# The last chunk of a mixture-of-experts layer: routed group in place of the dense form

## The chip, the cores and the metric

The kernel runs on one core of a Trainium2 chip. The metric is the device time of one execution in microseconds (us). Before the change the median of three executions is 1103.75 us (1101.72 to 1103.85).

## The reference

One transformer layer in float32 on x of 4 x 1024 tokens x 256 dims: causal attention over a window of 64 tokens (16 heads of 16 dims), residual and layernorm, then a mixture of experts, residual and layernorm.

```python
x = layernorm(x + attention(x))                      # x: (4, 1024, 256)
scores = sigmoid(x @ router_weight.T)                # 16 experts
sc = scores + e_bias                                 # top 2 of 4 groups, then
tidx = top_k(masked sc, 4)[1]                        # top 4 experts of a token
tw = 2.5 * scores[tidx] / sum(scores[tidx])
h = silu(x @ gate_w[e].T) * (x @ up_w[e].T)          # 256 -> 128, per expert
routed = sum over the 4 experts of tw * (h @ down_w[e].T)
shared = silu(x @ sg.T) * (x @ su.T) @ sd.T          # 256 -> 2 x 128
x = layernorm(x + routed + shared)
```

## The kernel before, in words

The 4096 tokens are 8 chunks (c) of 512 tokens, a chunk is 4 tiles of 128. Attention runs as 16 rounds of 13 slots. A planner, `plan()`, written in Python, gives every other job an integer half slot h on each of the five engines; each engine runs its jobs in order of h (`PE_AT`, `ACT_AT`, `DVE_AT`, `POOL_AT`, `SP_AT`) and waits on semaphores in between. Nothing is reordered at run time: a job that waits holds all that stands behind it on its engine. From `tail` = 416 on there are no attention slots, and the engines run only this list. Slots below are given relative to `tail`.

The experts are computed for groups of tokens. Groups 0, 1 and 2 are a batch of 8 tiles each, and group 3 is chunk 6 with 4 tiles. A routed group goes through these steps:

- `route` (5 parts) and `place` (5 parts) on DVE: top 4 of the experts and a row number for each of the token's four copies. Between them a `pos` job on PE (counts of tokens before each token).
- `scatter` on POOL: one indirect DMA per tile and rank, 16 for a group of 4 tiles, 32 for 8. It writes rows of the token in float16 pairs (high and low) into `rows[g % 2]` in DRAM. It waits until the last `gu` of group g - 2, which used the same buffer, is done.
- `load_rows` on SP: a transposing DMA of 256 rows, a pair of units. A unit is 128 rows of one expert; a group has 4 units per tile and 16 more for the rounding up, so 48 or 32 units, 24 or 16 pairs.
- `gu` on PE: 24 matmuls of 128 columns for a pair (gate and up, each in three float16 products). `tanh` (ACT), `gate` (DVE), `hh` (ACT) and `hl` (DVE) make the float16 pair of h, then `y` on PE: 6 matmuls of 256 columns. The planner puts `y` 7 slots behind its `gu` and holds five such pairs between them.
- `y_out` on ACT (into one of three `ys` buffers), `store_y` on SP into `outs[g % 2]` in DRAM.
- `gather` on POOL: one indirect DMA per tile and rank. It waits for all stores of its group, and for `comb_done` of the tile two before it, as there are two buffers `yg`.
- `combine` (4 dependent operations on a tile) and `stats2` on DVE; for each chunk `aggr2` (DVE), `rstd2` (POOL), `norm2` (ACT), `store` (SP).

The two shared experts of a group are `gu` and `ysh` jobs of 256 columns that need no scatter: they read `x1h` and `x1l` directly.

The last chunk, c = 7 (`DENSE`), is not routed to units: each of its tokens goes through all 16 experts and the 2 shared ones. `up` n is 12 matmuls of 512 columns, `dsilu`, `dgate` (times the weight of the expert, which `load_c` has spread over the partitions from `c_dram`), `dhi`, `dlo`, then `down` n, 12 matmuls of 256 columns that accumulate in two PSUM banks over all 18 experts. `residual` adds the sum to x1, and `aggr2` to `store` follow. There is nothing to scatter or to gather.

In the list the last `gu` of group 2 is at slot 38 and its last `y` at 45; group 3's routed pairs have `gu` from 48 to 83 and `y` from 55 to 90; `up` and `down` stand between them from 52 on, most of them behind; the gathers of group 2 are at 51 to 82 with `combine` at 58, 62, ... 86; those of group 3 are at 96 to 106. The list ends at slot 122.

Of the kernel before, what the change touches and what calls it, by code (L numbers as in the profile page):

```python
# [5 lines left out]
F32 = mybir.dt.float32  # L6
# [3 lines left out]
ALU = mybir.AluOpType  # L10
# [35 lines left out]
GROUPS = [(b, 0, BT) for b in range(B - 1)] + [(B - 1, 0, NT)]  # L46
DENSE = NC - 1
# [21 lines left out]
NCB = 4  # L69
NDH = 4  # L70
LAG = 2
# [43 lines left out]


def down(pe, dve, pool, act, sp, put, downs, h, w):

    n = downs.pop(0)
    h = put(("down", n), h)  # L120
    if n == NX - 1:
        at = max(h, w)
        dve[at + 1].append(("residual",))
        dve[at + 2].append(("aggr2", DENSE))
        pool[at + 3].append(("rstd2", DENSE))
        act[at + 4].append(("norm2", DENSE))
        sp[at + 5].append(("store", DENSE))
    return h


def plan():
# [40 lines left out]
    def chain(c, o, gap):  # L172
# [128 lines left out]
LO_POOL = ()  # L301
# [21 lines left out]
def attention_moe(nc, x, xT, winT, bqkT, bvr, woutT, bout, rwT, ebias, gwT, uwT, dwT, sgT, suT, sdT, out):  # L323
    with ExitStack() as ctx:
# [6 lines left out]
        c_dram = nc.dram_tensor("c_dram", [NE, CH], F32).ap()  # L331
# [11 lines left out]
        program(nc, ctx, banks, att, proj, moe, q_dram, k_dram, v_dram, c_dram, x1_dram, rows, outs, x, xT, winT, bqkT, bvr, woutT,  # L343
# [102 lines left out]
def program(nc, ctx, banks, att, proj, moe, q_dram, k_dram, v_dram, c_dram, x1_dram, rows, outs, x, xT, winT, bqkT, bvr, woutT, bout,  # L446
            rwT, ebias, gwT, uwT, dwT, sgT, suT, sdT, out):

    def sems(names, prefix):
# [23 lines left out]
    d = sems("""c_done cT_ready cT_done c_written c_loaded0 c_loaded1 c_loaded2 c_loaded3 up_ready silu_done sc_done h_done  # L473
        hi_done lo_done down_done z_done""", "d_")
    c_loaded = [d[f"c_loaded{i}"] for i in range(NCB)]
# [14 lines left out]
    cb = [flat[0].bitcast(F32)[:, i * CH:i * CH + CH] for i in range(NCB)]  # L490
    dhh, dhl = ([flat[1][:, (NDH * part + i) * CH:(NDH * part + i) * CH + CH] for i in range(NDH)] for part in range(2))
    cT = flat[2].bitcast(F32)[0:NE, 0:CH]
    dq, dga = ([PT[part][:, i, :] for i in range(2)] for part in range(2))
    dhf = [PT[part][:, 2, :] for part in range(2)]
# [3 lines left out]
    def rows_in(i):  # L498

        if i < LATE:  # L500
# [4 lines left out]
    cw = pick[:, DENSE % NH2 * NT:DENSE % NH2 * NT + NT, 0, :]  # L505
# [8 lines left out]
    RINGS = {"s_first": [0, 1, 2], "st_first": [3, 4, 5], "first": [7], "scores": [0, 1, 2, 3, 4], "other": [5, 7], "project": [5, 6, 7], "gates": [0, 1], "ups": [2, 3],  # L514
             "end": [5, 7, 0, 1, 2, 3], "sum0": [4], "sum1": [6]}
# [37 lines left out]
    def emptied(job):  # L553
# [49 lines left out]
    with nc.Block() as block:  # L603

        @block.tensor
        def _(pe):
# [97 lines left out]
            experts, sums = {}, []  # L704
# [14 lines left out]
            def fill(h):  # L719
# [59 lines left out]
                elif what == "cT":  # L779
                    on.wait_ge(d["c_done"], 1)  # L780
                    ps = take(ring, "cT")
                    for j in range(NT):
                        mm = pe.transpose(ps[0:NE, j * P:j * P + P], cw[:, j, :], ident[:])
                    mm.then_inc(d["cT_ready"], 1)
                elif what == "up":
                    n, = a
                    e, at = NE + n if n < NSH else n - NSH, DENSE % NH2 * CH
                    on.wait_ge(*x1_halves(DENSE))
                    on.wait_ge(s["w_lo"], NX)
                    for up, name in enumerate(("gates", "ups")):  # L790
                        ps = take(ring, name, n)
                        i = 0
                        for lo, xx in ((0, x1h), (0, x1l), (1, x1h)):
                            for k in range(KD):
                                mm = pe.matmul(ps[:], weights(e, (2 * up + lo) * D + k * P, P), xx[:, k, at:at + CH],  # L795
                                               start=(i == 0), stop=(i == 5))
                                i += 1
                        mm.then_inc(d["up_ready"], 1)
                elif what == "down":
                    n, = a  # L800
                    e = NE + n if n < NSH else n - NSH
                    on.wait_ge(d["lo_done"], n + 1)
                    if n == 0:
                        on.wait_ge(s["ot_done"], NR * NH2)
                        sums[:] = [take(f"sum{i}", "sum", i) for i in range(2)]
                    for j in range(NT):
                        y = sums[j // 2][:, j % 2 * D:j % 2 * D + D]
                        for i, (o, at) in enumerate(((dhh, 4 * D), (dhh, 5 * D), (dhl, 4 * D))):
                            mm = pe.matmul(y, o[n % NDH][:, j * P:j * P + P], weights(e, at, D),
                                           start=(n == 0 and i == 0 and j % 2 == 0), stop=(n == NX - 1 and i == 2),  # L810
                                           skip_group_check=True)
# [946 lines left out]
```

## Time and profile before

| what | us |
|---|---|
| median of three executions | 1103.75 |
| the profiled execution | 1103.76 |
| its span in the trace | 1102.0 |
| PE busy | 994.0 (90%) |
| DVE busy | 826.5 (75%) |
| ACT busy | 622.2 (56%) |
| POOL busy | 464.1 (42%) |

The device time of the profiled execution is 1.76 us above its span. A busy PE is not PE at its peak, since matmuls are pipelined and each is shown until it has drained. The profile gives for each line of the kernel and engine how long it was busy, and what ended the idle time before it. Instructions that issue a DMA from SP or POOL are shown with the time of the issue, not of the transfer.

### The profile page before, as it was taken

Reading aid. Unit: us, or ns where it says so; the run is one execution under the profiler, and the core shown is the slowest. Engines: PE = TensorE matmul, PEld = TensorE weight load, DVE = VectorE, ACT = ScalarE, POOL = GpSimd, SP = SyncE. Lnnn points to the kernel's source line nnn. Section 1 sums busy time; section 2 is a strip of 40 time slices with the busy share of each in tenths; the row PEclk is TensorE's granted clock in tenths of the full one; section 3 lists DMA queues with packets and bytes.
Section 4 is the critical chain, followed back from the end, with each engine's and each line's share of the span. In section 5 each row is a group of like instructions: output and inputs, shape, how many; then the busy total and the mean of one; then the engine's idle time right before and its main releaser. Section 6 shows DMA issues by size and latency. Waiting matters only on the chain.

```text
span 1102.0 us, 24714 instructions
## 1 busy us (share of the span) xinstructions
PE 994.0 (90%) x8538; PEld 574.0 (52%) x8538; DVE 826.5 (75%) x1824; ACT 622.2 (56%) x1418; POOL 464.1 (42%) x679
## 2 busy tenths in 40 slices
PE   8999999988888999998899988997998967999994
PEld 4554444444433455565564545564664546777662
DVE  8778888877887777778877888689776658457583
ACT  4336878676545666665466557664555754444322
POOL 8752221242128504120475665211556754246351
PEclk9999999999989999999999999999999988999997
DMA  5863356643113443543283866451446745899541
GB/s 186 264 220 98 125 176 212 224 119 83 49 43 112 110 97 92 115 116 65 83 183 125 174 154 160 80 119 40 119 153 134 200 108 158 185 196 239 179 140 39
DMA packets 216662, 150.73 MB, mean 137 GB/s; under 512 B 134608, under 2 KB 192720, under 8 KB 216544
## 3 DMA queue, kind: packets, MB, share of 16 engines
q1 hardware_dynamic: 204160, 116.63, 41.3%
q0 software_dynamic: 10752, 29.37, 8.7%
q10 hardware_dynamic: 1632, 3.15, 0.8%
q8 instruction: 75, 1.23, 0.5%
q14 instruction: 43, 0.35, 0.1%
HBM read 52.46 MB, written 70.29 MB: 111 GB/s over the span
## 4 chain that ended last, share of the span: by engine, by line
PE 53%; DVE 23%; POOL 6%; DMA 5%; issue 5%; ACT 5%; SPq 2%; DVEq 0%; ACTq 0%; POOLq 0%
PE bank L839 12%; PE bank L659 11%; PE bank L629 9%; PE bank L642 9%; DVE a_mx L1385 7%; DVE e_R L1679 4%; PE bank L852 3%; DMA a_pool<-outs,e_slot 2%; DMA k_dram<-p_qk 2%; PE bank L632 2%; PE bank L864 1%; PE bank L745 1%; ACT a_PT L1247 1%; POOL rows L1178 1%; ACT e_R L1301 1%
## 5 line engine op out<-in xcount | busy, mean ns | idle before, releaser
L1385 DVE TENSOR_REDUCE a_mx<-bank 128x1 f32<-128x512 f32 (+3 forms) x720 | 421.0, 618 | 140.1 <-PE bank L632 86.4
L1247 ACT ACTIVATE a_PT<-bank 128x512 f32<-128x512 f32 (+4 forms) x832 | 373.1, 497 | 176.8 <-PE bank L642 173.0
L642 PE MATMUL bank<-a_QS,a_KS 113*128 113x512 f16 (+4 forms) x832 | 272.0, 335 | 14.1 <-DVE a_mx L1385 13.3
L629 PE MATMUL bank<-a_KS,a_QS 112*128 112x512 f16 (+4 forms) x832 | 260.6, 334 | 13.9 <-DVE a_mx L1385 9.1
L1136 POOL TENSOR_SCALAR_AFFINE_SELECT a_PT<-a_PT 128x256 f32<-128x256 f32 (+1 forms) x288 | 112.2, 397 | 319.5 <-ACT a_PT L1247 318.8
L659 PE MATMUL bank<-a_PT,a_VG 128*17 128x512 f32 (+4 forms) x1664 | 182.7, 511 | 5.0 <-POOL a_PT L1136 4.9
L1178 POOL DMA_INDIRECT rows<-e_XR,e_slot x112 | 111.3, 993 | 108.2 <-DVEq L1537 80.0
L1186 POOL DMA_INDIRECT a_pool<-outs,e_slot x112 | 111.2, 993 | 84.5 <-DMA outs<-e_ys 32.6
L629 PEld LDWEIGHTS bank<-a_KS,a_QS 112*128 112x128 f16 x832 | 79.9, 98 | 114.0 <-ACT a_PT L1247 54.9
L642 PEld LDWEIGHTS bank<-a_QS,a_KS 113*128 113x128 f16 x832 | 81.1, 99 | 89.3 <-DVE a_mx L1385 35.2
L1331 ACT ACTIVATE e_tq<-bank 128x256 f32<-128x256 f32 x116 | 44.5, 384 | 143.2 <-PE bank L839 140.9
L839 PE MATMUL bank<-e_xt,a_W 128*128 128x128 f16 x1416 | 107.9, 225 | 8.4 <-DVE e_hf L1622 6.9
L632 PE MATMUL bank<-a_tri,a_idb 128*128 128x128 f16 (+1 forms) x576 | 110.6, 211 | 0.0
L839 PEld LDWEIGHTS bank<-e_xt,a_W 128*128 x1416 | 91.6, 100 | 29.7 <-issue 17.7
L852 PE MATMUL bank<-a_W,e_hh 128*128 x352 | 63.2, 276 | 7.5 <-DVE e_R L1669 3.4
L632 PEld LDWEIGHTS bank<-a_tri,a_idb 128*128 128x128 f16 x576 | 55.1, 99 | 27.8 <-issue 1.5
L1679 DVE SCALAR_TENSOR_TENSOR e_R<-a_pool,e_wk,e_R 128x256 f32<-128x256 f32 x112 | 57.8, 516 | 11.0 <-DMA a_pool<-outs,e_slot 8.0
L659 PEld LDWEIGHTS bank<-a_PT,a_VG 128*17 128x17 f32 x1664 | 33.8, 117 | 58.2 <-issue 45.3
L1629 DVE TENSOR_TENSOR e_hl<-e_hf,e_hh 128x256 f16<-128x256 f32 x116 | 49.7, 430 | 13.8 <-ACT e_hh L1338 11.8
L1338 ACT CAST e_hh<-e_hf 128x256 f16<-128x256 f32 x116 | 47.2, 408 | 19.3 <-DVE e_hf L1622 15.6
L1346 ACT ACTIVATE e_ys<-bank 128x512 f32<-128x512 f32 x88 | 52.2, 597 | 7.7 <-DMA outs<-e_ys 5.0
L795 PE MATMUL bank<-e_x1hl,a_W 128*128 128x512 f16 x216 | 49.4, 379 | 0.0
(178 smaller groups left out, 1323.6 us busy)
## 6 DMA issues: line engine op xcount, KB each, us to landing
outs<-e_ys SPq DMA_DIRECT2D x88, 256.0 KB, 3.8
rows<-a_pool SPq DMA_DIRECT2D x48, 256.0 KB, 3.6
q_dram<-p_qk SPq DMA_DIRECT2D x16, 256.0 KB, 2.8
k_dram<-p_qk SPq DMA_DIRECT2D x16, 256.0 KB, 4.0
v_dram<-p_vs SPq DMA_DIRECT2D x8, 512.0 KB, 7.3
a_QS<-q_dram SPq DMA_DIRECT2D x64, 64.0 KB
a_KS<-k_dram SPq DMA_DIRECT2D x64, 64.0 KB
a_VG<-v_dram SPq DMA_DIRECT2D x16, 256.0 KB, 4.2
```

What stands on the lines that cost most here:

```text
L629: mm = pe.matmul(ps[:, at:at + hi - lo], QS[p][0:MR, t // NT, h, t % NT * P:t % NT * P + P], KS[p][0:MR, piece, h % 2, 0:hi - lo], start=T ...
L632: mm = pe.matmul(ps[:, at + m0 - lo:at + hi - lo], idb[:], tri[:, m0 - P * t - WIN:m1 - P * t - WIN], start=False, stop=True)
L642: pe.matmul(ps[:, 0:(qc + 1) * CH - q0], KS[p][0:MR + 1, kt // NT, h % 2, kt % NT * P:kt % NT * P + P], QS[p][0:MR + 1, qc, h, q0 - qc * C ...
L659: mm = pe.matmul(otbank[32 * h:32 * h + HD + 1, q0 - qc * CH:CH], VG[p][:, kt, h:VW:HG], PT[(p + i) % 2][:, h, 0:(qc + 1) * CH - q0], star ...
L839: mm = pe.matmul(ps[:, up * 2 * P + at:up * 2 * P + at + v], weights(e, (2 * up + lo) * D + k * P, P), tall[k][part], start=(i == 0), stop ...
L852: mm = pe.matmul(ps[:, v * D:v * D + D], o[q % NHB][:, v * P:v * P + P], weights(e, at, D), start=(i == 0), stop=(i == 2))
L1136: pool.affine_select(out=a, in_=a, compare_op=ALU.is_ge, fill=0.0, base=q0 - (kt * P - WIN), pattern=[[0, 2], [1, w]], channel_multiplier= ...
L1178: pool.indirect_dma_start(rows[b % 2], bass.IndirectOffsetOnAxis(ap=slot[b % 3][:, at, k:k + 1], axis=0), XR[:, at, :], None).then_inc(sca ...
L1186: pool.indirect_dma_start(yg[i % 2][:, k, :], None, outs[b % 2], bass.IndirectOffsetOnAxis(ap=slot[b % 3][:, at, k:k + 1], axis=0)).then_i ...
L1247: act.activation(PT[(G + i) % 2][:, h, 0:w], bank("ST", G, i, h)[:, 0:w], ACT.Exp)\
L1385: dve.tensor_reduce(mx[:, piece, t // NT, heads[0]:heads[0] + n, t % NT], bank("S", G, u)[:, 0:n * w].rearrange("p (h k) -> p h k", h=n), ...
L1679: ins = dve.scalar_tensor_tensor(zz, yg[i % 2][:, k, :], wk[b % 3][:, at, k:k + 1], zz, op0=ALU.mult, op1=ALU.add)
```

## The change

Chunk 7 becomes group 4, a routed group of its own with 4 tiles in 32 units (16 pairs), built and run like group 3. The jobs `up`, `down`, `cT`, `dsilu`, `dgate`, `dhi`, `dlo`, `cTs`, `put_c`, `load_c`, `residual` and part 5 of `route` go, with their buffers and semaphores. Chunk 7 gets `row_hi` and `row_lo` (the float16 pair that is scattered), `pos`, `place`, scatters, gathers and combines. In the planner the routed pairs of group 4 are wanted only after the last one wanted of group 3, and the order of the jobs of groups 0 to 2 stays. The `end` ring of PSUM banks goes from six to seven.

```diff
-GROUPS = [(b, 0, BT) for b in range(B - 1)] + [(B - 1, 0, NT)]
-DENSE = NC - 1
+GROUPS = [(b, 0, BT) for b in range(B - 1)] + [(B - 1, half * NT, NT) for half in range(NH2)]
...
-        if c != DENSE:
-            act[y + 6].append(("row_hi", c))
-            pool[y + 7].append(("row_lo", c))
+        act[y + 6].append(("row_hi", c))
+        pool[y + 7].append(("row_lo", c))
...
-    sp[tail - 14].append(("load_res", DENSE))
-    pool[tail - 10].append(("add_bo", DENSE))
-    ready[DENSE], at = chain(DENSE, tail + 3, 1)
-    for n in range(RPARTS + 1):
-        dve[at + 2 + n].append(("route", NGR, n))
-    at = put(("cT",), at + RPARTS + 4)
-    act[at + 1].append(("cTs",))
-    sp[at + 2].append(("put_c",))
-    weighed = at + 3
-
     wanted, order = [], {}
+    for g in range(NGR):
+        lo = max(routed[g] + 5, max((h for h, *_ in wanted[-1:]), default=0) + 1 if g == NGR - 1 else 0)
+        hi = routed[g + 1] - 7 if g < B - 2 else LEFT + tail if g == B - 2 else lo + SPACE * NPR[g]
+        wanted += [(lo + (hi - lo) * n // NPR[g], g, NPS[g] + n) for n in range(NPR[g])]
     for g in range(NGR):
         for n in range(NPS[g]):
             c, tile = shared_place(g, n)
             wanted.append((ready[c] + tile * 5, g, n))
-        lo = routed[g] + 5
-        hi = routed[g + 1] - 7 if g < B - 2 else LEFT + tail if g == B - 2 else lo + SPACE * NPR[g]
-        wanted += [(lo + (hi - lo) * n // NPR[g], g, NPS[g] + n) for n in range(NPR[g])]
...
-    h, downs = ready[DENSE] + 1, []
-    for n in range(NX):
-        h = max(h + 1, ready[DENSE]) if n < NSH else max(h + 1, weighed + 1)
-        h = put(("up", n), h)
-        act[h + 1].append(("dsilu", n))
-        dve[h + 1].append(("dgate", n))
-        act[h + 1].append(("dhi", n))
-        (pool if n in LO_POOL else dve)[h + 2].append(("dlo", n))
-        if n >= NSH:
-            sp[h - 2 if n < NSH + NCB else h - 1].append(("load_c", n - NSH))
-        downs.append(n)
-        if len(downs) > LAG:
-            down(pe, dve, pool, act, sp, put, downs, h, w + 6)
-    while downs:
-        h = down(pe, dve, pool, act, sp, put, downs, h + 1, w + 6)
...
-    RINGS = {"s_first": [0, 1, 2], "st_first": [3, 4, 5], "first": [7], "scores": [0, 1, 2, 3, 4], "other": [5, 7], "project": [5, 6, 7], "gates": [0, 1], "ups": [2, 3],
-             "end": [5, 7, 0, 1, 2, 3], "sum0": [4], "sum1": [6]}
+    RINGS = {"s_first": [0, 1, 2], "st_first": [3, 4, 5], "first": [7], "scores": [0, 1, 2, 3, 4], "other": [5, 7], "project": [5, 6, 7], 
+             "end": [5, 7, 0, 1, 2, 3, 4]}
...
-                _, j0, n = GROUPS[r] if r < NGR else (B - 1, DENSE % NH2 * NT, NT)
+                _, j0, n = GROUPS[r]
```

## Rows read from the trace of the kernel before

**Rows 1.** Busy time of each engine by stretch, then PEclk, DMA share, GB/s.

```profile
900.00:905.00 5.00, 3.42 (x21) 3.02 (x20) 2.33 (x6) 3.92 (x8) 1.56 (x3) 0.50 0.26 82
...
980.00:1000.00 20.00, 19.44 (x199) 14.61 (x198) 12.28 (x29) 7.79 (x18) 9.54 (x11) 1.00 0.97 179
...
1040.00:1060.00 20.00, 19.52 (x121) 11.49 (x119) 14.18 (x24) 6.33 (x12) 11.83 (x11) 1.00 0.65 193
```

**Rows 2.** Waits from 940 to 1102 us: total, times, longest.

```profile
POOL a_pool L1186 <- DMA outs<-e_ys: 32.6, 2, 24.5
```

**Rows 3.** PE in order of time: start, length, line, shape, count, idle time before.

```profile
912.21 0.64 PE L852 MATMUL bank<-a_W,e_hh 128*128 x2
...
937.26 2.24 PE L839 MATMUL bank<-a_KS,a_W 128*128 128x128 f16 x24 [0.91 <-issue]
...
953.33 6.60 PE L839 MATMUL bank<-a_KS,a_W 128*128 128x128 f16 x72
...
968.48 1.50 PE L839 MATMUL bank<-a_PT,a_W 128*128 128x128 f16 x24
...
1028.13 1.47 PE L809 MATMUL bank<-a_W,a_QS 128*128 128x256 f16 x12
1029.44 2.75 PE L795 MATMUL bank<-e_x1hl,a_W 128*128 128x512 f16 x12
...
1032.58 0.27 PE L852 MATMUL bank<-a_W,e_hl 128*128 x1
```

**Rows 4.** POOL in order of time: scatters L1178, gathers L1186.

```profile
926.35 1.12 POOL L1178 DMA_INDIRECT rows<-e_XR,e_slot  x1 [0.75 <-DVEq L1537]
...
945.70 0.96 POOL L1178 DMA_INDIRECT rows<-e_XR,e_slot  x1 [0.30 <-issue]
971.17 0.98 POOL L1186 DMA_INDIRECT a_pool<-outs,e_slot  x1 [24.52 <-DMA outs<-e_ys]
...
1022.23 1.07 POOL L1186 DMA_INDIRECT a_pool<-outs,e_slot  x1 [0.30 <-issue]
...
1043.12 1.08 POOL L1186 DMA_INDIRECT a_pool<-outs,e_slot  x1 [8.04 <-DMA outs<-e_ys]
...
1066.46 0.95 POOL L1186 DMA_INDIRECT a_pool<-outs,e_slot  x1 [0.30 <-issue]
```

**Rows 5.** DVE in order of time: combines L1679.

```profile
1028.71 2.04 DVE L1679 SCALAR_TENSOR_TENSOR e_R<-a_pool,e_wk,e_R 128x256 f32<-128x256 f32 x4 [2.62 <-DMA a_pool<-outs,e_slot]
...
1053.58 2.04 DVE L1679 SCALAR_TENSOR_TENSOR e_R<-a_pool,e_wk,e_R 128x256 f32<-128x256 f32 x4
...
1070.90 2.04 DVE L1679 SCALAR_TENSOR_TENSOR e_R<-a_pool,e_wk,e_R 128x256 f32<-128x256 f32 x4
```

**Rows 6.** ACT in order of time: norm2 L1307, y_out L1346.

```profile
1035.11 2.08 ACT L1307 ACTIVATE e_R<-e_R,e_nm,e_rstd 128x256 f32<-128x256 f32 x4 [0.82 <-POOL e_nm L1147]
...
1039.67 0.59 ACT L1346 ACTIVATE e_ys<-bank 128x512 f32<-128x512 f32 x1
```

**Rows 7.** DVE in order of time, near the end: `bn_stats` of chunk 7.

```profile
1089.97 1.39 DVE L1662 BATCH_NORM_STATS2 e_st<-e_R 128x6 f32<-128x256 f32 x4
```

**Rows 8.** The page's costliest groups: `hh`, which stands for `tanh`, `gate` and `hl` too.

```profile
L1338 ACT CAST e_hh<-e_hf 128x256 f16<-128x256 f32 x116 | 47.2, 408 | 19.3 <-DVE e_hf L1622 15.6
```

**Rows 9.** Lines of `row_hi` and `row_lo`: duration min/median/max in ns, then first start.

```profile
L1281 ACT CAST e_XR<-e_R x7: 1027/1038/1067, 234.6 to 903.6; 128x1024 f16<-128x1024 f32 x7
...
L1168 POOL TENSOR_TENSOR e_XR<-e_R,e_XR x7: 2130/2132/2325, 236.7 to 904.7; 128x1024 f16<-128x1024 f32 x7
```

**Rows 10.** DMA queues from 980 to 1000 us: packets, MB, share of 16 engines.

```profile
q1 hardware_dynamic: 5974, 2.49, 67.6%
q0 software_dynamic: 379, 1.03, 28.7%
```

**Rows 11.** The same from 1043 to 1060 us.

```profile
q1 hardware_dynamic: 1064, 1.93, 37.6%
q0 software_dynamic: 473, 1.30, 25.4%
```

More of the change, by code:

```diff
@@ L114, in shared_place @@
     return chunk_of(g, n // NSH * 2), n // NSH * 2 % NT
[L117 to L128, printed above, removed]
 def plan():
@@ L300 @@
 SPACE = 2
-LO_POOL = ()
 PPARTS = 5
@@ L342, in attention_moe @@
         moe = expert_memory(opener(ctx, "e_"))
[L343 removed]
+        program(nc, ctx, banks, att, proj, moe, q_dram, k_dram, v_dram, x1_dram, rows, outs, x, xT, winT, bqkT, bvr, woutT,
                 bout, rwT, ebias, gwT, uwT, dwT, sgT, suT, sdT, out)
@@ L489, in program @@
     x1_loaded = [f["x1_loaded0"], f["x1_loaded1"]]
[L490 to L494, printed above, removed]
     late_tiles = [a.rearrange("p (k t) -> p k t", k=4) for a in (flat[2][:, 2 * CH:4 * CH], flat[3][:, 0:2 * CH],
@@ L778, in fill @@
                     mm.then_inc(f["pos_ready"], 1)
[L779 to L811, printed above, removed]
-                    mm.then_inc(d["down_done"], 1)
                 elif what == "gu":
@@ L1031, in fill @@
                           .then_inc(y_stored[i % 3], 16)
-                    elif what == "put_c":
-                        on.wait_ge(d["cT_done"], 1)
-                        sp.dma_start(c_dram, cT).then_inc(d["c_written"], 16)
-                    elif what == "load_c":
-                        e, = a
-                        on.wait_ge(d["c_written"], 16)
-                        on.wait_ge(s["st_ready"], (NR - 1) * NST)
-                        on.wait_ge(s["s_ready"], (NR - 1) * NU)
-                        on.wait_ge(d["sc_done"], e - NCB + 1)
-                        sp.dma_start(cb[e % NCB], c_dram[e, :].partition_broadcast(P)).then_inc(c_loaded[e % NCB], 16)
                     elif what == "store":
@@ L1491, in route @@
                                            op=ALU.is_equal))
-                    if r == NGR:
-                        link(dve.tensor_reduce(cw, kk.rearrange("p t k e -> p t e k"), AX.X, ALU.add))
-                        return
                     on.wait_ge(f["pos_ready"], r)
@@ L1630, in fill @@
                             .then_inc(f["hl_done"], 1)
-                    elif what == "dlo":
-                        n, = a
-                        on.wait_ge(d["hi_done"], n + 1)
-                        on.wait_ge(d["down_done"], n - NDH + 1)
-                        on.wait_ge(s["st_ready"], NR * NST)
-                        dve.tensor_tensor(dhl[n % NDH], dhf[n % 2], dhh[n % NDH], op=ALU.subtract)\
-                            .then_inc(d["lo_done"], 1)
-                    elif what == "dgate":
-                        n, = a
-                        on.wait_ge(d["silu_done"], n + 1)
-                        g = dq[n % 2]
-                        if n >= NSH:
-                            e = n - NSH
-                            on.wait_ge(c_loaded[e % NCB], (e // NCB + 1) * 16)
-                            on.wait_ge(d["h_done"], n - 1)
-                            g = dga[n % 2]
-                            dve.tensor_tensor(g, dq[n % 2], cb[e % NCB], op=ALU.mult).then_inc(d["sc_done"], 1)
-                            on.wait_ge(d["sc_done"], e + 1)
-                        on.wait_ge(d["up_ready"], 2 * n + 2)
-                        on.wait_ge(d["lo_done"], n - 1)
-                        dve.scalar_tensor_tensor(dhf[n % 2], bank("ups", n)[:], 1.0 / WSC, g, op0=ALU.mult, op1=ALU.mult)\
-                            .then_inc(d["h_done"], 1)
-                    elif what == "residual":
-                        on.wait_ge(d["down_done"], NX)
-                        for i in range(2):
-                            zz = x1_of(DENSE)[:, 2 * i:2 * i + 2, :].rearrange("p j n -> p (j n)")
-                            dve.scalar_tensor_tensor(zz, bank("sum", i)[:], 1.0 / WSC, zz, op0=ALU.mult, op1=ALU.add)\
-                               .then_inc(d["z_done"], 1)
-                        for i in range(2):
-                            on.wait_ge(d["z_done"], i + 1)
-                            for j in range(2 * i, 2 * i + 2):
-                                dve.bn_stats(st[1][:, j, :], x1_of(DENSE)[:, j, :]).then_inc(f["stats2_done"], 1)
                     elif what == "add_shared":
```

47 lines of the change are left out of this document (3 added, 44 removed).

## The prediction, made before the change was run

> **What bounds the kernel now.** The change touches nothing that is ordered before the last chunk's work, so I read only what lies behind 900 us, first by stage. The busy times say that PE is full and its clock is at the upper level from 980 to 1060 us, while the DMA share falls from 0.97 to 0.65 [rows 1]. Before that fall the routed pairs run, behind it the dense chunk, which needs little DMA. Next the waits: what the gathers on POOL wait for longest is the stores of `y`, 24.5 us before the gathers of group 2 and 8.0 before those of group 3 [rows 2, 4]. That idle time costs nothing now, because PE has the dense chunk to do: an `up` and a `down` take 1.31 + 2.59 us, read from the start of one to the start of the next [rows 3], and PE ends with them. Group 3's last `y` ends at 1032.85 [rows 3], its last combine at 1072.94 [rows 5], both in the shade of the dense work. So now the end is set by PE's matmuls, plus one short chain behind the last `down`: from the end of `bn_stats` at 1091.36 it is 10.6 us to the end of the span [rows 7].
>
> **The change, part by part.**
>
> *What goes.* 18 `up` and 18 `down` on PE, 18 x 3.9 = 70 us, and with them the DVE and ACT work per expert and the DMAs of 16 `load_c` and one `put_c`.
>
> *What comes on PE.* Four shared `gu` and two `ysh` of 12 matmuls of 256 columns. A `down` has the same form, 1.31 us, so 6 x 1.31 = 7.9. Then 16 pairs. A `gu` takes 2.2 us (72 matmuls in 6.60 for three) and at best, behind a backlog, 1.34 to 1.50 [rows 3]; a `y` is half a `down`, 0.66. From 937.26 to 959.93 there are eight `gu` and six `y`: 22.7 less 4.0 is 2.34 a `gu`, 3.0 a pair. 16 pairs are 48 us (bounds 32 and 48). PE thus saves 70 - 7.9 - 48 = 14 us. If PE still set the end, `y` of the last pair would be done at 968.5 (the start of group 3's first routed `gu` [rows 3]) + 8 shared jobs x 1.31 + 32 pairs x 3.0 = 1075.
>
> *What comes behind it.* A routed group ends with a store of `y`, a round of gathers, and combines. That is the serial part that the dense form did not have, and it is exposed at the end, as nothing is left to run beside it. The rest of the sum is a relay of three rounds, because POOL and DVE run their lists in order.
>
> 1. *Scatters of group 4.* They write to the buffer of group 2 and so wait for its last `gu`, which ends at 959.93 [rows 3]. POOL was idle there, from 946.66 to 971.17. Group 3's 16 scatters took 20.3 us [rows 4], so these end at 980.2, and the gathers of group 2, behind them on POOL, start 9 us later than their 971.17. All before 959.93 is covered: `route`, `pos` and `place` of group 4 run some 15 us earlier. `row_hi` and `row_lo`, 1.04 us on ACT and 2.1 on POOL [rows 9], fall before the idle stretch of POOL and cost nothing; without that cover they would be 3 us.
> 2. *Round of group 2.* First gather to last combine took 971.17 to 1030.75, 59.6 us [rows 4, 5]. POOL's own pace (31 intervals of 1.27, one `rstd2`, landing and combine) would give 48. I take 58, since the dense `dgate` and `dlo` no longer stand between the combines on DVE: 1038.2. `gate` and `hl` of the pairs wait behind these combines. By the planner's rule group 3's last `hl` now stands behind the last combine of group 2 (slots 89 and 86; before, both at 86, `hl` first). PE alone would be at that `y` about 1036, so DVE is late, not PE.
> 3. *To the gathers of group 3.* `norm2` of chunk 5 stands on ACT before the last two `y_out`. It ended 6.4 us behind the last combine of group 2 [rows 5, 6]; add 0.6 for one `y_out`, and 3.45 from the start of the last `y_out` to the first gather (1039.67 to 1043.12 [rows 4, 6]): 10.5, so 1048.7.
> 4. *Round of group 3*: 1043.12 to 1072.94, 29.8 us [rows 4, 5]. The arithmetic agrees: a tile is 4 gathers x 1.27, a combine came 6.5 us behind the start of its last gather where it waited for the DMA (1022.23 to 1028.71), and with two buffers that gives 29.9. It ends at 1078.5.
> 5. *Last pairs of group 4.* That combine is at slot 112, the `hl` of the last four pairs at 114 to 120. Again `norm2` (6.4), then `tanh`, `gate`, `hh`, `hl` at 0.41 [rows 8], `y` 0.66, `y_out` and store 3.45, and 0.5 for handoffs: 12.6, so 1091.1. PE alone would have let these gathers start at about 1079.
> 6. *Round of group 4.* Bounds 29.9 with the landing above and 25.7 with 4.4 us, the most that it can have been for group 3's last tile (1066.46 to 1070.90 [rows 4, 5]). The DMA queues are nearly idle by then, so 27: 1118.1.
> 7. *The end.* One `bn_stats` (0.42) and the 10.6: 11.1. Span 1129.2.
>
> The span of the profiled execution is 1.76 us short of its device time, which stands 0.01 above the median. So 1131.0, 27 us slower than 1103.75.
>
> The combine that waited for its DMA began 5.4 us behind the end of the issue (1023.30 to 1028.71 [rows 4, 5]). The Trainium skill, *DMA: Bandwidth & Descriptors*, section "Anatomy of one DMA — SWDGE (gpsimd) path", states a fixed cost of about 2.0 us plus the bytes; for 128 KB that is an estimated 2.3 us behind the issue, and by that estimate the last round would be 24.3 us and the whole 1128.
>
> **The rivals.**
>
> *Rounds at POOL's pace.* If landings are short, the round of group 2 takes 48 (1028.2), group 3's gathers start at 1038.7 and its combines end about 1064; then the relay has let go and PE's 1075 counts: + 3.6 + 25.7 + 11.1 = 1115.4, 1117 in device time. For it: only 4.4 us at most in the last round. Against it: combines of group 2 did wait for the DMA. The fixed cost that the Trainium skill gives on its DMA page, named above, would lead here too.
>
> *DMA becomes the bound.* From 1043 to 1060 eleven gathers took 25.4% and six loads of 256 KB 37.6% of 17 us, 0.39 and 1.07 us each [rows 11]. From 980 to 1000 the queue with six transposing loads and five plain transfers was busy 13.5 us [rows 10], so a transposing load is 1.36. Group 4's stage of some 48 us asks 16 x (1.36 + 1.07) + 16 x 0.39 and two outputs at about 2: 49 us. It is as full as the chip's queues go, and `y_out` waits for its buffer. If each round is longer by a tenth and the last pairs by 3 us, 1131 + 5.8 + 3 + 2.7 + 3 = 1145.
>
> *PE's clock falls.* At 900 to 905 PE was busy 3.42 of 5 us and the granted clock 0.50, that is 1.2 GHz; two matmuls of 256 columns then took 0.64 us in place of 0.38 [rows 1, 3]. With the dense work gone PE has pauses of that sort behind 1030. A `y` would be 1.3, a `gu` 2.6; twelve `gu` and sixteen `y` from 1040 end at 1092 instead of under the relay's 1087: 1136. The Trainium skill, *TensorE: Matmul & The Clock Gate*, section "What's actually happening", says that the throttled clock is the default and activity lifts it; the row at 900 us agrees, and by that rule the sum would be this 1136.
>
> *Faster.* The other side: no job waits behind a combine, and pairs run at 2.25 us, between the 2.0 of a backlog and 3.0. Then the last `y` is at 968.5 + 10.5 + 72 = 1051, and + 3.6 + 25.7 + 11.1 + 1.8 = 1093. This decides under 2.5 us a pair. For it: `gu` of 1.5 us do occur [rows 3]. Against it: those are behind an `up` or shared job, which gives the queue its backlog, and rounds at POOL's own pace with the handoffs between them give 1117 by themselves.
>
> **How the numbers follow.** The relay as summed 0.50 (1123 to 1138), POOL's pace 0.24 (1108 to 1122), DMA bound 0.13 (1138 to 1152), clock 0.06 (1136), faster 0.07, about half of it under 1101.5, the rest from there to 1108. The range that leaves out no more than 2 in 10 is 1108 to 1147. A measurement of this kernel tells 0.2%, 2.2 us, from no change. Faster by more 0.05, within 0.03, slower 0.92.
>
> **What would show it.** The first gather of group 2 at about 980 and 16 scatters before it; combines of group 3 ending near 1078; `gate` and `hl` waiting for combines; PE with idle stretches behind 1020; four tiles of gathers with nothing beside them in the last 38 us. The forecast is wrong if gathers of group 2 start at 971, if the last `y` ends before 1080, or if the last round is under 24 us.

## The result, and the profile after

The changed kernel takes 1133.87 us (median of four, 1131.96 to 1142.67) beside 1103.8 us (four, 1101.72 to 1109.49) for the kernel before: 1.0274 times as long, 95% interval 1.0243 to 1.0304, or 30 us more. The profiled execution took 1132.21, with a span of 1130.4. The forecast was 1131.0, in a range of 1108 to 1147.

The page first: the span, then busy time of each engine.

```profile
span 1130.4 us, 25405 instructions
...
PE 981.4 (87%) x8659; PEld 574.2 (51%) x8659; DVE 821.7 (73%) x1841; ACT 623.7 (55%) x1438; POOL 493.7 (44%) x712
```

PE has 12.6 us less to do than before (994.0), and the kernel is still 30 us longer. So the added time is time in which PE's matmuls don't run. The busy time by stretch, with PEclk, DMA share and GB/s behind the engines, says where:

```profile
980.00:1000.00 20.00, 15.56 (x196) 13.59 (x194) 8.49 (x20) 4.39 (x13) 15.38 (x16) 1.00 0.93 198
1000.00:1020.00 20.00, 18.40 (x196) 14.83 (x193) 11.39 (x31) 9.12 (x23) 14.37 (x17) 0.92 1.08 232
...
1060.00:1080.00 20.00, 17.74 (x186) 13.48 (x186) 10.44 (x25) 6.59 (x15) 10.78 (x12) 1.00 1.02 240
1080.00:1100.00 20.00, 6.80 (x52) 4.03 (x49) 4.95 (x16) 7.08 (x16) 5.63 (x8) 0.71 0.34 112
1100.00:1130.00 30.00, 0.00 (x0) 0.00 (x0) 9.84 (x24) 2.07 (x4) 13.06 (x16) 0.50 0.24 75
```

The last two lines are the new tail: PE, the first number behind the length, works 6.80 of 20 us and then not at all for 30; its last `y` ends at 1090.96. Before, it worked to 1088.72 of 1102.0 us: to 1081.68, and then, after a wait of 2.79 us for a `dlo`, the last two `down`.

```profile
1084.47 4.25 PE L809 MATMUL bank<-a_W,a_QS 128*128 128x256 f16 x24 [2.79 <-DVE a_QS L1636]
```

Further up PE is no longer full (15.56 where it was 19.44 [rows 1]), and the DMA share stays near 1 up to 1080, where it had fallen to 0.65 [rows 1]. The relay can be read off POOL's timeline, which answers to [rows 4]: the first scatter of group 4, its last, and the first gather of groups 2, 3 and 4, then the last gather.

```profile
965.55 0.95 POOL L1071 DMA_INDIRECT rows<-e_XR,e_slot  x1 [14.68 <-PE bank L742]
...
986.16 0.96 POOL L1071 DMA_INDIRECT rows<-e_XR,e_slot  x1 [0.30 <-issue]
987.44 0.99 POOL L1079 DMA_INDIRECT a_pool<-outs,e_slot  x1 [0.31 <-issue]
...
1054.26 1.08 POOL L1079 DMA_INDIRECT a_pool<-outs,e_slot  x1 [10.59 <-DMA outs<-e_ys]
...
1095.13 1.08 POOL L1079 DMA_INDIRECT a_pool<-outs,e_slot  x1 [10.35 <-DMA outs<-e_ys]
...
1114.07 0.95 POOL L1079 DMA_INDIRECT a_pool<-outs,e_slot  x1 [0.30 <-issue]
```

The brackets tell what ended each wait: PE's last `gu` of group 2 for the scatters, nothing but POOL's own order for the gathers of group 2, and the stores of `y` for those of groups 3 and 4. DVE's combines answer to [rows 5]: the first and last of group 2, the last of group 3, the first and last of group 4.

```profile
994.83 2.07 DVE L1512 SCALAR_TENSOR_TENSOR e_R<-a_pool,e_wk,e_R 128x256 f32<-128x256 f32 x4 [8.64 <-DMA a_pool<-outs,e_slot]
...
1037.88 2.04 DVE L1512 SCALAR_TENSOR_TENSOR e_R<-a_pool,e_wk,e_R 128x256 f32<-128x256 f32 x4
...
1079.27 2.04 DVE L1512 SCALAR_TENSOR_TENSOR e_R<-a_pool,e_wk,e_R 128x256 f32<-128x256 f32 x4
...
1101.82 2.04 DVE L1512 SCALAR_TENSOR_TENSOR e_R<-a_pool,e_wk,e_R 128x256 f32<-128x256 f32 x4 [12.47 <-DMA a_pool<-outs,e_slot]
...
1116.81 2.04 DVE L1512 SCALAR_TENSOR_TENSOR e_R<-a_pool,e_wk,e_R 128x256 f32<-128x256 f32 x4 [2.36 <-DMA a_pool<-outs,e_slot]
```

What stands between them shows in the waits from 940 to 1131 us (total, times, longest). The wait of [rows 2] has become 20.9 us, and four others stand beside it:

```profile
DVE e_R L1512 <- DMA a_pool<-outs,e_slot: 45.1, 12, 12.5
...
POOL a_pool L1079 <- DMA outs<-e_ys: 20.9, 2, 10.6
...
ACT e_ys L1222 <- DMA outs<-e_ys: 17.1, 12, 3.0
POOL rows L1071 <- PE bank L742: 14.7, 1, 14.7
...
PE bank L755 <- DVE e_hl L1494: 9.8, 6, 3.9
```

The forecast and the trace, leg by leg; the end of one leg is the start of the next:

| leg | ends, forecast | ends, measured | length, forecast | length, measured |
|---|---|---|---|---|
| last `gu` of group 2 | 959.9 | 964.7 | - | - |
| to the first gather of group 2 | 980.2 | 987.4 | 20.3 | 22.7 |
| round of group 2 | 1038.2 | 1039.9 | 58 | 52.5 |
| to the gathers of group 3 | 1048.7 | 1054.3 | 10.5 | 14.3 |
| round of group 3 | 1078.5 | 1081.3 | 29.8 | 27.1 |
| to the gathers of group 4 | 1091.1 | 1095.1 | 12.6 | 13.8 |
| round of group 4 | 1118.1 | 1118.9 | 27 | 23.7 |
| end of the span | 1129.2 | 1130.4 | 11.1 | 11.5 |

### The profile page after: what moved, and what is told of

It is laid out like the page before. It is cut to its first block, busy times and chain, and to the rows that moved or that the text cites. A ratio compares the mean times of both kernels' runs of the same rounds, so it can differ in the third digit from the quotient of the medians.

```text
span 1130.4 us, 25405 instructions
## 1 busy us (share of the span) xinstructions
PE 981.4 (87%) x8659; PEld 574.2 (51%) x8659; DVE 821.7 (73%) x1841; ACT 623.7 (55%) x1438; POOL 493.7 (44%) x712
## 4 chain that ended last, share of the span: by engine, by line
PE 50%; DVE 22%; POOL 9%; issue 6%; DMA 6%; ACT 4%; SPq 2%; DVEq 0%; ACTq 0%; POOLq 0%
PE bank L596 11%; PE bank L742 11%; PE bank L566 9%; PE bank L579 9%; DVE a_mx L1261 7%; POOL a_pool L1079 4%; DVE e_R L1512 3%; PE bank L755 3%; DMA a_pool<-outs,e_slot 2%; POOL rows L1071 2%; DMA outs<-e_ys 2%; PE bank L569 2%; PE bank L682 1%; DMA k_dram<-p_qk 1%; PE bank L767 1%
## 5 line engine op out<-in xcount | busy, mean ns | idle before, releaser
L1071 POOL DMA_INDIRECT rows<-e_XR,e_slot x128 | 126.9, 991 | 129.8 <-DVEq L1402 81.1
L1079 POOL DMA_INDIRECT a_pool<-outs,e_slot x128 | 124.9, 976 | 69.4 <-issue 31.8
L1207 ACT ACTIVATE e_tq<-bank 128x256 f32<-128x256 f32 x136 | 51.6, 383 | 142.0 <-PE bank L742 140.4
L1512 DVE SCALAR_TENSOR_TENSOR e_R<-a_pool,e_wk,e_R 128x256 f32<-128x256 f32 x128 | 65.6, 513 | 51.6 <-DMA a_pool<-outs,e_slot 48.2
L755 PE MATMUL bank<-a_W,e_hh 128*128 x416 | 78.0, 283 | 17.5 <-DVE e_hl L1494 9.8
L1214 ACT CAST e_hh<-e_hf 128x256 f16<-128x256 f32 x136 | 55.2, 407 | 52.5 <-DVE e_hf L1480 36.2
L1494 DVE TENSOR_TENSOR e_hl<-e_hf,e_hh 128x256 f16<-128x256 f32 x136 | 57.9, 428 | 28.5 <-ACT e_hh L1214 24.4
L1222 ACT ACTIVATE e_ys<-bank 128x512 f32<-128x512 f32 x104 | 61.8, 597 | 20.0 <-DMA outs<-e_ys 17.1
L755 PEld LDWEIGHTS bank<-a_W,e_hh 128*128 128x128 f16 x416 | 39.0, 99 | 44.8 <-issue 33.6
```

Source lines behind the costliest of these rows:

```text
L755: mm = pe.matmul(ps[:, v * D:v * D + D], o[q % NHB][:, v * P:v * P + P], weights(e, at, D), start=(i == 0), stop=(i == 2))
L1071: pool.indirect_dma_start(rows[b % 2], bass.IndirectOffsetOnAxis(ap=slot[b % 3][:, at, k:k + 1], axis=0), XR[:, at, :], None).then_inc(sca ...
L1079: pool.indirect_dma_start(yg[i % 2][:, k, :], None, outs[b % 2], bass.IndirectOffsetOnAxis(ap=slot[b % 3][:, at, k:k + 1], axis=0)).then_i ...
L1512: ins = dve.scalar_tensor_tensor(zz, yg[i % 2][:, k, :], wk[b % 3][:, at, k:k + 1], zz, op0=ALU.mult, op1=ALU.add)
```

## The experiments

The theory is the relay of the forecast: three rounds of gathers and combines, each behind the one before through POOL's and DVE's order, and the last with nothing beside it. The rivals are PE's pace, the DMA queues, and the loss of the backlog that the dense jobs gave to PE.

**The last round taken away.** POOL gathers nothing for group 4 (first piece of the diff) and DVE combines nothing (second); chunk 7's sum leaves out the routed experts. The normalisation waits for the stores of `y` in their place.

```diff
+                        if b == NGR - 1:
+                            continue
...
+                        if b == NGR - 1:
+                            for n in range(3):
+                                on.wait_ge(y_stored[n], (ROUTED_TO[b + 1] + 2 - n) // 3 * 16)
+                            continue
```

> The changed kernel without the gathers and combines of group 4; its output leaves out the routed experts of the last chunk. Relay theory: the last round of gathers stands alone at the end, 23.7 us from 1095.1 to 1118.9, and nothing takes its place, so the time falls by 23 to 24 us to about 1109 (ratio to before 1.004). Rival, the loss comes from the matmuls of the pairs or from the DMA queues before 1090: the round is replaced by some other late work, the time falls by under 10 us.

1110.45 us (1108.29 to 1114.47), ratio 1.0044 [1.0023, 1.0065]: by the medians 23.4 us less than with the round, as expected; the span is 1108.7, 21.7 less. What is left ends like this:

```profile
1094.83 0.60 ACT L1224 ACTIVATE e_ys<-bank 128x512 f32<-128x512 f32 x1 [0.57 <-DMA outs<-e_ys]
1097.65 1.41 DVE L1525 BATCH_NORM_STATS2 e_st<-e_R 128x6 f32<-128x256 f32 x4 [5.11 <-DMA outs<-e_ys]
```

By the spans, 21.7 of the 28.4 us that the change cost are this one round; the last `y_out` starts 3.2 us later here than in the changed kernel (1091.65), so it may be a little more. Without the round the changed kernel is still not faster than the one before, although its PE has 12.6 us less to do: its last `y_out` starts at 1094.83, where the last `down` of the kernel before ended at 1088.72.

**A third buffer for the scatters.** Group 4 scatters into a `rows` buffer of its own, so its scatters wait for no `gu`. The buffer needs 16 more `fill_rows`, which stand far earlier.

```diff
-        rows = [nc.dram_tensor(f"rows{i}", [ROWS, 2 * D], F16).ap() for i in range(2)]
+        rows = [nc.dram_tensor(f"rows{i}", [ROWS, 2 * D], F16).ap() for i in range(3)]
...
-                        if b >= 2:
+                        if 2 <= b < 4:
...
-                        pool.indirect_dma_start(rows[b % 2], bass.IndirectOffsetOnAxis(ap=slot[b % 3][:, at, k:k + 1],
+                        pool.indirect_dma_start(rows[b % 2 if b < 4 else 2], bass.IndirectOffsetOnAxis(ap=slot[b % 3][:, at, k:k + 1],
```

> The changed kernel with a third buffer for scattered rows, so that group 4's scatters need not wait for group 2's last gate and up matmuls. Relay theory: the 16 scatters fill POOL's idle time from 951 to 971, the gathers of group 2 start about 975 in place of 987, all three rounds move and the time falls by 7 to 12 us. Rival, PE or the DMA queues pace the stretch to 1095: group 2's gathers start earlier but the last y of group 4 does not, the time falls by under 3 us.

1128.39 us (1126.08 to 1128.77), ratio 1.0195 [1.0153, 1.0237]: 5.5 us less by the medians, between the 7 to 12 of the relay and the rival's 3; the span is 1126.8. POOL's timeline shows the last scatter, now 14 us earlier, and the first gather of group 2 behind it:

```profile
972.14 0.96 POOL L1071 DMA_INDIRECT rows<-e_XR,e_slot  x1 [0.30 <-issue]
979.44 0.99 POOL L1079 DMA_INDIRECT a_pool<-outs,e_slot  x1 [6.34 <-DMA outs<-e_ys]
```

The gathers start 8.0 us earlier, now held by the stores of `y`. But the round that follows lasts from 979.44 to 1038.03, 58.6 us in place of 52.5, so only 1.9 us of the 8.0 are left at its end, and 3.6 in the span. The DMA share from 980 to 1040 is 1.03, 1.08 and 1.23. The chain that the profile follows back from the end runs mostly through PE's `gu` and `y` here from 970 to 1026, where in the changed kernel it runs through POOL's scatters and gathers up to 1006. A step that comes earlier is worth only what the next round can take up.

**Two combines behind the last `hl`.** The combines of group 3's tiles 2 and 3 stand behind the last `hl` of group 4 on DVE, so that the last pairs don't wait for them.

```diff
             w = at + steps_of(g, t * TOPK + TOPK) + 3
+            if g == B - 1 and t >= 2:
+                w = last[NGR - 1] - 5 + t
```

> The changed kernel with the last two combines of group 3 ordered on DVE behind the last hl of group 4. Relay theory: the last four pairs no longer wait for the gathers of group 3 and the last gathers start 5 to 9 us earlier, so the time falls by as much. Rival, the DMA queues pace the last pairs (loads and stores of y): the time falls by under 2 us.

1131.11 us (1126.86 to 1134.24), ratio 1.0213 [1.0164, 1.0263], which overlaps the interval of the changed kernel; the 5 to 9 us expected are not there. In the profiled execution the relay was already 6.5 us late at the gathers of group 3, so its span of 1132.4 says little; the length from there to the gathers of group 4 does:

```profile
1060.74 1.08 POOL L1081 DMA_INDIRECT a_pool<-outs,e_slot  x1 [10.40 <-DMA outs<-e_ys]
...
1097.20 1.08 POOL L1081 DMA_INDIRECT a_pool<-outs,e_slot  x1 [0.61 <-issue]
```

36.5 us in place of 40.9. The wait for the stores is gone from the last bracket; what holds the gathers now is the late combines themselves (the last ends at 1093.52) and `rstd2` of chunk 6, which stands before the gathers on POOL and for which POOL stood 11.62 us. So the combines in front of the last `hl` cost 4.4 us of this leg in the one trace, and moving them opens the next bound at once.

**A filler on PE.** Four matmuls of 512 columns with no use stand before each of the 16 routed `gu` of group 4.

```diff
+                    if b == NGR - 1 and n >= NPS[b]:
+                        for _ in range(4):
+                            pe.matmul(ps[:], idb[:], woh[:].rearrange("p k d -> p (k d)"), start=True, stop=True)
```

> The changed kernel with four idle matmuls of 512 columns ahead of each routed gate and up job of group 4, 0.85 us of PE work a pair, 13.6 us for the 16. Relay theory: PE has slack there, since the last pairs wait for combines, so the time rises by 0 to 5 us. Rival, PE's work sets the end of the pairs: it rises by 11 to 14 us.

1138.51 us (1135.45 to 1143.26), ratio 1.0313 [1.0283, 1.0344], which overlaps the interval of the changed kernel. The profile lists the addition on PE from 1020 to 1100 us, and PE's timeline shows one block of it with the `gu` behind:

```profile
L739 PE MATMUL bank<-a_woh,a_idb 128*128 128x512 f16 x64 | 16.4, 378 | 2.8 <-issue 1.6 <-ACT e_ys L1225 1.2
```

```profile
1037.21 1.03 PE L739 MATMUL bank<-a_woh,a_idb 128*128 128x512 f16 x4
1038.08 1.50 PE L745 MATMUL bank<-a_KS,a_W 128*128 128x128 f16 x24
```

The span (1133.5) is 3.1 longer and the median 4.6, within the 0 to 5 of the relay. But this test is weaker than it was meant to be. The `gu` behind a block takes 1.50 us in place of 2.1, so the block gives back most of what it costs: from 1020 to 1100 PE is busy 63.35 us where it was 60.30, 3.1 more and not 16.4. A PE that set the end would have passed on about as much as was seen. What speaks on PE is the chain that the profile follows back from the end. For the changed kernel from 1030 us on it has this, and its last piece of PE ends at 964.8:

```profile
by line: POOL a_pool L1079 20.0%; DMA a_pool<-outs,e_slot 14.6%; DMA outs<-e_ys 14.5%; issue 13.5%; DVE e_R L1512 9.6%; ACT e_R L1200 4.7%; ACT e_ys L1222 3.3%; POOL e_rstd L1037 3.1%; SPq L927 2.7%; DVE e_hf L1480 1.8%; DVE e_mv L1525 1.0%
```

So PE wasn't the last to be waited for, though not far from it, as the third buffer showed.

**Fewer bytes.** `y` of groups 3 and 4 is stored and gathered as float16, which rounds the routed sum of the last two chunks.

```diff
...
-                        act.mul(ys[i % 3][:].rearrange("p v d -> p (v d)"), bank("y", *a)[:], 1.0 / WSC)
+                        to = half_ys(i).rearrange("p v d -> p (v d)") if a[0] >= 3 else ys[i % 3][:].rearrange("p v d -> p (v d)")
+                        act.mul(to, bank("y", *a)[:], 1.0 / WSC)
```

> The changed kernel with y of groups 3 and 4 stored and gathered as float16 (rounded, which changes the last bits of the result): 32 stores and 32 gathers move half the bytes, some 17 + 6 us less of the DMA queues' time. Rival that the DMA queues pace the pairs from 1000 to 1090 us: the waits of y_out for its buffer (17.1 us) go, the last y comes earlier, 6 to 12 us faster than the changed kernel. Relay theory with DMA only as landing time: 1 to 3 us faster.

1129.19 us (1128.42 to 1133.18), ratio 1.0223 [1.0193, 1.0252]: 4.7 us less by the medians, with intervals that just overlap, and 2.5 by the spans (1127.9). By the spans that is the 1 to 3 of the relay, by the medians it lies between them and the rival's 6 to 12. In the busy time by stretch the DMA share has fallen from 0.91 and 1.02 to 0.81 and 0.76:

```profile
1040.00:1060.00 20.00, 18.73 (x194) 14.24 (x193) 7.80 (x24) 10.93 (x27) 5.65 (x9) 1.00 0.81 164
1060.00:1080.00 20.00, 19.28 (x204) 14.61 (x203) 12.36 (x29) 6.21 (x15) 11.42 (x12) 1.00 0.76 149
```

The round of group 3 shrinks from 27.1 to 24.3 us (1054.84 to 1079.17), and the last round, where the queues are idle in any case, stays what it was, 24.0. The DMA queues have a part in the middle of the relay; halving what they move for `y` doesn't remove the relay.

**Four edits together**: the third buffer, the late combines, float16 `y`, and `norm2` of chunks 5 and 6 eight slots later.

> The changed kernel with the third buffer of rows, the two combines behind the last hl, norm2 of chunks 5 and 6 eight slots later, and y of groups 3 and 4 as float16. Relay theory: each handoff is shorter and the time falls to 1110 to 1117, still above the kernel before because the last round stands alone. Rival, one resource paces all: no better than the best of the edits alone, 1120 and above.

1120.94 us (1120.2 to 1123.8), ratio 1.0149 [1.0124, 1.0173]. The expected 1110 to 1117 is missed: this is the rival's 1120 and above, though 7 us below the best of the edits alone. It is the shortest routed form here, and still 1.5% behind the kernel before. Its last stretch, and the first gather of the last round on POOL:

```profile
1080.00:1119.00 39.00, 0.00 (x0) 0.00 (x0) 10.27 (x28) 4.15 (x8) 18.97 (x24) 0.51 0.17 54
```

```profile
1083.09 1.08 POOL L1090 DMA_INDIRECT a_pool<-half,e_slot  x1 [0.61 <-issue]
```

PE has nothing left at 1080, and the round runs from 1083.09 to 1106.84, 23.7 us again. Of the 12.0 us that the span lost against the changed kernel, all lie in front of the last round. From 1020 to 1090 us, 58% of the chain followed back from the end is PE's `gu` and `y` in this run: with the handoffs shortened PE is the next bound, which the relay of the forecast left out.

**The kernel before, with the dense jobs spread.** Nine of the `up`, where it was six, stand 7 slots apart among the routed pairs of groups 2 and 3, from slot 25 on, with their `down` behind them.

```diff
+SPREAD_UPS, SPREAD_BY, SPREAD_AT = 9, 7, 25
...
+    for n in range(SPREAD_UPS):
+        h = up_at(n, SPREAD_AT + tail + SPREAD_BY * n)
+        if len(downs) > LAG:
+            put(("down", downs.pop(0)), h + 2)
...
```

> The kernel before, with nine of the dense up jobs placed every seventh slot among the routed pairs of groups 2 and 3 in place of six. Theory: matmuls of 128 columns come at the pace of issue, 2.2 us for 24, and at 1.4 behind a dense job, so each up that is moved among them saves about 1.2 us: 3 to 5 us faster than the kernel before (ratio 0.996). Rival: what is saved is lost by dgate and dlo standing between gates and combines on DVE, and the end is 0 to 4 us later.

1104.5 us (1101.93 to 1107.57), ratio 0.9993 [0.9971, 1.0015]: no difference, where 3 to 5 us less were expected. PE's timeline shows an `up` and then `gu` at both paces:

```profile
1010.55 2.75 PE L805 MATMUL bank<-e_x1hl,a_W 128*128 128x512 f16 x12
1013.14 1.50 PE L849 MATMUL bank<-a_KS,a_W 128*128 128x128 f16 x24
...
1016.45 1.50 PE L849 MATMUL bank<-a_KS,a_W 128*128 128x128 f16 x24
...
1018.50 2.15 PE L849 MATMUL bank<-a_KS,a_W 128*128 128x128 f16 x24
```

So a `gu` right behind an `up` is shorter, 1.50 in place of 2.15, but nothing was won: group 3's gathers started at 1063.83 (before, 1043.12 [rows 4]), and PE waited 4.4 us for DVE's `dlo` in four times and 1.3 for a bank that `dgate` frees, where it was 3.3 in two times and none. The longest of these waits, 2.71 us before the last `down`, is the 2.79 of the kernel before. That backlog is real, and a form with more of it is no faster.

**The kernel before, with float16 `y`** for groups 2 and 3.

> The kernel before with y of groups 2 and 3 as float16 (rounded). If the full DMA queues hold the routed pairs up from 930 to 1010 us there too, PE reaches the dense chunk earlier and the time falls by 3 to 6 us. If PE's own pace counts, it falls by under 1.5 us.

1103.62 us (1099.89 to 1109.53), ratio 0.9987 [0.9969, 1.0005]: 1.2 us less by the medians, which is no difference that can be told, where the same edit took 4.7 off the changed kernel. By the spans of the profiled executions the two gains are alike, 2.9 and 2.5 us. PE is busy 20.00 of 20 us from 1040 on:

```profile
1040.00:1060.00 20.00, 20.00 (x126) 12.12 (x124) 16.04 (x28) 6.90 (x12) 13.20 (x13) 1.00 0.50 153
```

That fits dense work that covers the transfers, but the contrast between the two kernels isn't large enough to show it.

**Three runs on another chip.** They shared a chip on which the kernel before took 1185.32 us, so they are compared with each other and not with those above. The first moves `norm2` and the store of chunks 5 and 6 eight slots later, the second has this, the third buffer and the late combines with `y` in float32, the third is the changed kernel.

```diff
-                act[w + 4].append(("norm2", c))
-                sp[w + 5].append(("store", c))
+                late = 8 if c in (5, 6) else 0
+                act[w + 4 + late].append(("norm2", c))
+                sp[w + 5 + late].append(("store", c))
```

> The norm2 step, the store of the sum and the reload of chunks 5 and 6 stand eight slots later in the unit order; nothing else differs from the changed kernel. Theory (relay: what delays the gathers of groups 3 and 4 is the leg from the last combine to the last y_out, in which VectorE's 2.08 us norm2 and the sum's store and reload lie between): 1 to 4 us less than the changed kernel, 1128 to 1133, ratio 1.022 to 1.026. Rival (the leg waits for the y_out buffers, that is for the DMA traffic of the e_ys stores, and norm2 hides in it): no change, ratio 1.027.

> The third rows buffer, the two combines behind the last hl and the norm2 step eight slots later, together, with y kept in float32. Relay theory: the three edits take 4 to 14 us off the changed kernel together, 1118 to 1129, ratio 1.013 to 1.022; it stays slower than before because the last round of 23.7 us stands in all of them. Rival (DMA order absorbs all that starts earlier, so that only the float16 y of the four-edit kernel opened it): no better than the third rows buffer alone, ratio 1.0195.

> The changed kernel once more, unchanged, on the chip of the two runs above, to compare them on one chip: 1130 to 1134, ratio 1.024 to 1.030.

The changed kernel took 1233.09 us (1228.9 to 1235.37), ratio 1.0413 [1.0374, 1.0451]; with `norm2` late 1232.15 (1224.16 to 1236.76), 1.0396 [1.0349, 1.0443]; with the three edits 1227.16 (1221.94 to 1234.92), 1.0377 [1.0328, 1.0425]. All intervals overlap. All expected times missed, since they were made for the other chip, and so did the expected ratios. Against the changed kernel on the same chip, `norm2` late is 0.9 us shorter by the medians, which is no difference, and the three edits are 5.9 shorter, in the expected 4 to 14 but not clear of noise. The traces say more. The first gather of group 4, in the changed kernel and with `norm2` late:

```profile
1191.78 1.08 POOL L1079 DMA_INDIRECT a_pool<-outs,e_slot  x1 [10.34 <-DMA outs<-e_ys]
```

```profile
1196.44 1.08 POOL L1080 DMA_INDIRECT a_pool<-outs,e_slot  x1 [8.68 <-DMA outs<-e_ys]
```

From the end of group 3's last combine (1177.96 and 1184.28) that is 13.8 and 12.2 us, and in front of group 3's gathers 13.4 and 12.2. By these two traces `norm2` in that place costs 1.2 to 1.6 us of a leg, somewhat under its own 2.08; the times can't tell it. The last round takes 23.7 us in each of the three, as on the first chip.

## Why the forecast came out

**The total.** It is right for the reason given: PE's saving is real (14 us forecast, 12.6 measured in its busy time) and bought nothing, since the end moved to a serial round that the dense form didn't have. The first experiment shows the round, 21.7 us of 28.4 in the span; that PE wasn't the last to be waited for in front of it rests on the chain of the profile, not on the filler. That 1131 came so near to 1134 is luck in part: the legs were off by up to 5.5 us and cancelled, 4.8 + 2.4 - 5.5 + 3.8 - 2.7 + 1.2 - 3.3 + 0.4 = 1.1.

**The kernel before.** The forecast read its end as set by PE's matmuls, with group 3's last combine "in the shade of the dense work". That isn't quite so. The last two `down` waited 2.79 us for `dlo`, and the chain behind that wait runs back over ACT, where `norm2` of chunk 6 stands in front (1079.04 to 1081.11), to group 3's combines. They then took 4.25 us together, where two took 2.6 before, at a granted clock of 0.67 from 1084 to 1089. The sum doesn't use this reading, since it starts from the legs behind 959.93.

**Step 1, the scatters of group 4.** The wait is the one named, 14.7 us for the last `gu` of group 2. That `gu` ended at 964.7 in place of 959.9. What was wrong is "All before 959.93 is covered: `route`, `pos` and `place` of group 4 run some 15 us earlier". They do run earlier, on a DVE that was already busy, and PE waits for it: 2.1 us were lost by group 3's `pos` (922.56, before 920.49), 2.0 more at chunk 7's router scores (L701), and 0.5 at its `pos`.

```profile
936.53 0.26 PE L701 MATMUL bank<-a_rwh,e_x1hl 128*128 128x16 f16 x4 [2.01 <-DVE e_x1hl L1468]
...
945.36 0.21 PE L711 MATMUL bank<-a_M,a_before 128*128 128x80 f16 x1 [0.50 <-DVEq L1363]
```

And the leg from there to the first gather was 2.4 longer, with 0.8 us to the first scatter and 2.7 between the first two. The bigger error is what I made of it: I counted each us of delay through to the end. The third buffer gave the gathers 8.0 us and the end 3.6, so the delay at the scatters isn't worth its size.

**Step 2, the round of group 2.** 52.5, not 58. I had kept it near the 59.6 of before; it was only 4.5 above the 48 of POOL's own pace. With the third buffer the same round took 58.6 and ended at about the same time, so it has no length of its own to be taken from a row. The trace of the changed kernel says what its end waited for. The last combine (1037.88) has no wait for its gather; DVE had stood 3.43 us for `hh` of a pair, and on ACT that `hh` stood behind a `y_out` that waited for its buffer, for the store of an earlier pair. The chain in order of time:

```profile
1030.15 6.05 DMA outs<-e_ys
1036.28 0.60 ACT e_ys L1222
1036.88 0.30 ACT e_hh L1214
...
1037.55 0.42 DVE e_hf L1480
1037.97 0.40 DVE e_R L1512
```

With the third buffer DVE waits 3.67 us for `hh` in the same place. How long the gather had been there by then isn't shown.

**Steps 3 and 5, the legs to the next gathers.** 14.3 and 13.8 for 10.5 and 12.6. What was missing is the wait of `y_out` for its buffer, that is for the store of three pairs before: 17.1 us in 12 times, of which 2.4 and 1.2 us stand in these two legs. I had it in the rival "DMA becomes the bound" and not in the sum. The `norm2` was in the sum and belongs there, with the 1.2 to 1.6 us that the traces of the other chip show for it.

**Step 4.** 27.1 for 29.8. I had every combine 6.5 us behind the start of its last gather, from one row of before; here it was 5.5, 5.7, 6.6 and 4.3.

**Step 6, the last round.** 23.7, below my lower bound of 25.7, and in my own list a last round "under 24 us" was to speak against the forecast. The term was mis-sized: I took the landing as at most 4.4 us from a row with other transfers beside it. Here the last gather starts at 1114.07 and its combine at 1116.81, 2.7 us later, and all 16 gathers ran at POOL's 1.25 us. The estimate of 24.3 from the Trainium skill, *DMA: Bandwidth & Descriptors*, section "Anatomy of one DMA — SWDGE (gpsimd) path", was the nearer one; here the combine came 1.8 us behind the end of the issue, where the page led to an estimated 2.3.

**The rivals.** *POOL's pace*: true of the last round alone; it needed the round of group 2 at 48 us, and that took 52.5. *DMA as the bound*: true in part. The share was 0.91 to 1.1 from 980 to 1080 and float16 `y` gave 2.5 us by the spans, 4.7 by the medians, but the rounds got shorter and not longer, and the last one doesn't touch it. Its price of 1.07 us a load divides the queue's time by six loads, while the 1.93 MB beside it [rows 11] are those of more than seven; by bytes a load is nearer 0.87. *PE's clock*: it didn't come about. The granted clock stood at 0.91 to 1.00 in each stretch of 20 us up to 1080. It did fall for a short time behind three pauses: 0.50 from 1000 to 1002, behind one of 3.92 us; 0.66 and 0.77 from 1033 to 1039, behind 1.53; and 0.59 from 1088 to 1091, behind 3.03, where the last two `y` took 2.7 us in place of 1.3. The `y_out` behind these two waited for stores and not for PE. The rule that I quoted from the Trainium skill, *TensorE: Matmul & The Clock Gate*, section "What's actually happening", names the direction, and these rows agree with it. The rival had the lower level from 1040 on, and from there to 1080 the rows show the upper one. *Faster*: it asked for pairs under 2.5 us. `gu` without a backlog took 2.0 to 2.3, as forecast, and a job did wait behind the combines: PE stood 3.92 us for `hl` while DVE waited 8.64 for the gathers.

**What stays open.** The length of the middle rounds is shared between DVE's order, the stores of `y`, the loads and, as soon as these are shortened, PE. The third buffer and float16 `y` moved the span by 3.6 and 2.5 us, the four edits by 12.0, and no run took one of the four away altogether. The chain of a profile names only the last of the things waited for, and in this stage they are near to each other. On the other chip the change cost 47.8 us in place of 30. The last combine of group 3 to the end is 49.1 there and 49.1 here, so the rest lies further up; since there is no trace of the kernel before from that chip, I can't say how it divides.

## What to carry to other kernels

When work is taken from the engine that looks full, ask what its jobs were covering. Here 70 us of dense matmuls hid two rounds of gathers and combines but for 2.8 us; their replacement needs less of PE but ends with a serial round, 16 gathers x 1.25 us and a landing, that nothing covers. So compare the forms of a last stage by the chain behind the last matmul too, and not by the matmuls alone: it is 13.3 us in the dense form (1088.72 to 1102.0) and 39.4 in the routed one (1090.96 to 1130.4). When filling an engine to see whether it has slack, look at how much its busy time really grew, 3.1 us here for 16.4 put in. A saving at the front of such a relay counts for what the next round can take up, 3.6 of 8.0 us here.

## What the hardware showed that I had not expected

**The landing of a gather depends on what else the queues carry far more than on its size.** With the queues well used, 5.4 us from the end of the issue to the combine in the kernel before [rows 4, 5]; with them idle 1.8, for the same 128 KB. With 64 KB (float16 `y`, group 4) it is 1.6, from 1112.75 to 1114.32.

**One chip was 7% slower on the same program, and not through a lower clock alone.** The kernel before took 1185.32 us there for 1103.8, at a mean granted clock of 0.95 for 0.97. In the changed kernel PE stood still there in stretches in which it waited for nothing that the profile shows. The waits of PE there, from 1000 us on, with "issue" as the releaser:

```profile
PE bank L742 <- issue: 18.2, 26, 2.5
PE bank L767 <- issue: 14.0, 11, 3.0
PE bank L755 <- issue: 11.7, 18, 1.2
```

That is 43.9 us; on the first chip the same stage, from 940 on, had 6.8. The stretch with the longest of these pauses, with PE's busy time, PEclk, DMA share and GB/s:

```profile
1050.00:1060.00 10.00, 1.70 (x5) 0.50 0.37 102
```

PE ran five matmuls in 10 us at the lower clock, all of one `ysh` job that had begun at 1043.17. What holds the instructions back isn't in the trace.
